# Selective-scan kernel: delta and delta*u spread by fp32 matmuls of 32 rows instead of packed bf16 parts

## What is computed

```python
s0, s1 = xf[..., diag], xf[..., anti]              # two orders of the 4096 positions
xs = jnp.stack([s0, s1, s0[..., ::-1], s1[..., ::-1]], axis=1)      # 4 directions, 192 channels
x_dbl = jnp.einsum('bkdl,kcd->bkcl', xs, x_proj_weight)
dts, Bs, Cs = jnp.split(x_dbl, [6, 22], axis=2)
delta = jax.nn.softplus(einsum('bkrl,kdr->bkdl', dts, dt_projs_weight) + dt_projs_bias)
def step(hst, inp):
    u_t, d_t, B_t, C_t = inp
    hst = hst * jnp.exp(d_t[..., None] * A) + (d_t * u_t)[..., None] * B_t[:, :, None, :]
    return (hst, jnp.einsum('bkdn,bkn->bkd', hst, C_t))
```

## Time and profile before

| | us |
|---|---|
| median of 3 runs | 16992.62 (16989.31 to 17001.06) |
| span of the profiled execution, first to last instruction | 16982.4 |
| busy: VectorE / TensorE / GpSimd / ScalarE | 14254.2 / 11990.6 / 9441.8 / 8240.7 |
| mean granted TensorE clock | 0.73 of full speed |

### The profile page before, as it was taken

One profiled execution on the slowest core, in us unless ns is written; L12 is line 12 of the kernel. 1 busy time (PEld: TensorE's weight loads), 2 busy tenths in 40 slices (PEclk: granted clock), 3 DMA queues, 4 the chain that ended last, 5 costly groups with the idle time before them and its releaser, 6 DMA issues.

```text
span 16982.4 us, 206915 instructions
## 1 busy us (share of the span) xinstructions
PE 11990.6 (71%) x50304; PEld 4377.0 (26%) x50304; DVE 14254.2 (84%) x15991; ACT 8240.7 (49%) x15277; POOL 9441.8 (56%) x4852
## 2 busy tenths in 40 slices
PE   6766777667776677766777667776677766777667
PEld 2222322223222242222422223222232222322224
DVE  6999579995799947999479995799957999579994
ACT  4555445554455534555345554455544555445553
POOL 4666346663466634666346663466634666346662
PEclk8777677776777767777677776777767777677776
DMA  1111011110111101111011110111101111011110
GB/s 31 34 33 33 17 28 33 33 33 17 27 34 33 33 17 27 34 33 33 17 27 34 33 33 17 27 33 33 33 18 27 33 33 33 19 26 33 33 33 15
DMA packets 523906, 485.87 MB, mean 29 GB/s; under 512 B 160703, under 2 KB 457312, under 8 KB 523052
## 3 DMA queue, kind: packets, MB, share of 16 engines
q1 hardware_dynamic: 523052, 476.64, 13.1%
HBM read 27.61 MB, written 12.58 MB: 2 GB/s over the span
## 4 chain that ended last, share of the span: by engine, by line
DVE 33%; issue 31%; PE 20%; ACT 7%; POOL 4%; DVEq 3%; POOLq 1%; DMA 0%; SPq 0%; ACTq 0%
DVE ps L1131 11%; DVE arena L1166 8%; PE ps L775 5%; DVE arena L1124 4%; DVE arena L1095 3%; DVE arena L1098 2%; DVE arena L1085 2%; POOL arena L467 2%; PE ps L937 2%; PE ps L936 2%; ACT arena L629 2%; PE ps L915 1%; DVE arena L1117 1%; PE ps L805 1%; POOL arena L424 1%
## 5 line engine op out<-in xcount | busy, mean ns | idle before, releaser
L467 POOL TENSOR_TENSOR arena<-arena 128x1024 f32<-128x1024 f32 x3072 | 7363.4, 2413 | 4072.1 <-PE ps L867 3764.3
L1166 DVE TENSOR_TENSOR_SCAN arena<-arena,ps 128x512 f32<-128x512 f32 x6144 | 7723.6, 1257 | 8.2
L629 ACT ACTIVATE arena<-ps,negA 128x512 f32<-128x512 f32 x6144 | 4130.8, 684 | 6261.1 <-PE ps L828 6244.4
L825 PE MATMUL ps<-arena,spread 96*128 96x512 bf16 x6144 | 2923.2, 476 | 4059.1 <-DVE arena L1166 3994.4
L1131 DVE TENSOR_TENSOR ps<-ps,arena 128x512 f32<-128x512 f32 x6144 | 4145.6, 675 | 44.3 <-PE ps L825 35.1
L867 PE MATMUL ps<-arena,gather 128*32 128x256 f32 x24576 | 3076.9, 472 | 9.5 <-POOL arena L467 9.3
L828 PE MATMUL ps<-arena,spread 96*128 96x512 bf16 x6144 | 2949.2, 480 | 12.9 <-ACT arena L629 12.9
L825 PEld LDWEIGHTS ps<-arena,spread 96*128 96x128 bf16 x6144 | 623.0, 101 | 7353.7 <-DVE arena L1166 4746.7
L424 POOL TENSOR_TENSOR arena<-arena 128x512 f32<-128x512 f32 x512 | 651.1, 1272 | 1037.7 <-ACT arena L571 1037.7
L867 PEld LDWEIGHTS ps<-arena,gather 128*32 128x32 f32 x24576 | 676.5, 119 | 1958.5 <-issue 1922.7
L805 PE MATMUL ps<-u_lo,xw_lo 128*128 (+2 forms) x1520 | 1003.7, 760 | 83.1 <-DVEq L163 54.4
(11 more groups left out here) (178 smaller groups left out, 11564.8 us busy)
## 6 DMA issues: line engine op xcount, KB each, us to landing
arena<-arena SPq DMA_DIRECT2D x3072, 96.0 KB, 2.2
arena<-arena SPq DMA_DIRECT2D x512, 256.0 KB, 5.0
arena<-in_x SPq DMA_DIRECT2D x128, 192.0 KB, 3.2
out_tokens<-arena SPq DMA_DIRECT2D x64, 192.0 KB, 2.2
arena<-in_cw SPq DMA_DIRECT2D x1, 648.0 KB
xw_lo<-in_xbc_lo SPq DMA_DIRECT2D x1, 256.0 KB
xw_hi<-in_xbc_hi SPq DMA_DIRECT2D x1, 256.0 KB
arena<-in_spread SPq DMA_DIRECT2D x1, 192.0 KB
```

The costliest lines, as they stand in the source:

```text
L467: pool.tensor_tensor(wgt[s % RW], hst[s % RH], c_rep[ch.par].unsqueeze(1).to_broadcast([P, 2, T]), ALU.mult).then_inc(weighted, 1)
L629: act.activation(decay[s % RDA][:, a, :], bank(3 + a), ACT.Exp, scale=negA[:, ch.k, group(s, a):group(s, a) + 1]).then_inc(decay_ready, 1)
L825: pe.matmul(bank(q % 3), spread[:, i, :], to_du[:, 2 * j + a, :], start=True, stop=True).then_inc(du_ready, 1)
L1166: dve.tensor_tensor_scan(hst[s % RH][:, a, flip], decay[s % RDA][:, a, flip], bank(q % 3)[:, flip], 0.0 if kind == 0 else state[:, q:q + 1 ...
```

## The change

- The tiles `delta_lo`, `du_lo` and `mixed` are doubled (by `ch.par`) and stay fp32. The parts, their splitting on VectorE, GpSimd and ScalarE, and the 12 packing DMAs are gone.
- `fill_du` and `fill_delta` take the place of `fill`: for a step, two fp32 matmuls of 32 rows each, which read the 32 channels where they lie. A tile's block of 32 channels selects the row group of the array. Even and odd steps take the two halves of the lo channels in turn, and a du fill runs one step behind the delta fill, so the two read different row groups; the hi channels come in the last four steps.
- PSUM: du in banks 0, 1 and 2, 3 by turns, delta in 4 and 5, y of lo and of hi one after the other in bank 6. `carry` for hi waits until lo is saved.
- `make_delta` reads the maximum from bank 7 instead of SBUF. `mix_du` moves to GpSimd, at its step 10, on all 128 partitions; `other_rows` waits for it.
- Gather matmuls have 512 columns instead of 2 x 256, in other places (`SUMS`); VectorE multiplies both groups of a step, then scans both.
- Rings: decays 4 steps instead of 2, weighted states 6 instead of 4; decays are issued two steps ahead.

Core of the diff:

```diff
-        SUMS = {4: (0, 1), 7: (2, 3), 8: (4,), 9: (5,), 11: (6, 7), 13: (8, 9), 14: (10,), 15: (11,)}
+        LO_STEPS = 8
+        SUMS = {3: (0, 1), 5: (2, 3), 7: (4, 5), 9: (6, 7), 11: (8, 9), NSTEP + 1: (10, 11)}
+        DU_BANKS, DELTA_BANK, Y_BANK = (0, 2), 4, 6
+        def step(ch, s):
+            return (s // 2, (s + 1 - ch.dir) % 2) if s < LO_STEPS else (s - LO_STEPS, 2)
...
+                def mix_du(ch):
+                    pool.wait_ge(delta_done, ch.n(2, 2))
...
+                    pool.tensor_tensor(mixed[ch.par], t_l, u_hi[:, bass.ds(ch.t0, T)], ALU.mult).then_inc(mixed_done, 1)
...
                 def other_rows(ch):
-                    act.wait_ge(delta_done, ch.n(2, 2))
-                    if not ch.first:
-                        act.wait_ge(split_last, ch.n(2, 0))
+                    act.wait_ge(mixed_done, ch.n(2, 1))
...
-                def fill(ch, q):
...
-                    pe.matmul(bank(q % 3), spread[:, i, :], to_du[:, 2 * j + a, :], start=True, stop=True).then_inc(du_ready, 1)
...
+                def fill_du(ch, s):
...
+                    if not (ch.first and s < 2):
+                        pe.wait_ge(scan_done, ch.n(NGRP, 2 * (s - 2) + 2))
+                    for a in range(2):
+                        tile, row = (du_lo, 32 * (2 * j + a)) if j < 2 else (mixed, ch.r0 + 32 * a)
+                        pe.matmul(bank(DU_BANKS[s % 2] + a), spread[row:row + 32, i, :], tile[ch.par][row:row + 32, :],
+                                  start=True, stop=True).then_inc(du_ready, 1)
+                def fill_delta(ch, s):
...
+                    if not (ch.first and s < 1):
+                        pe.wait_ge(decay_ready, ch.n(NGRP, 2 * (s - 1) + 2))
...
+                def carry(ch, z):
+                    if z == 1:
+                        wait_apart(pe, y_saved, ch.n(2, 1))
...
+                        if s + 2 < NSTEP:
+                            fill_du(ch, s + 2)
+                        elif nx:
+                            fill_du(nx, s + 2 - NSTEP)
+                        if s + 3 < NSTEP:
+                            fill_delta(ch, s + 3)
+                        elif nx:
+                            fill_delta(nx, s + 3 - NSTEP)
+                        if s in (3, 11):
+                            carry(ch, s // 11)
...
+                        if nx and s in (0, 5):
+                            project(nx, s // 5, 0)
+                            project(nx, s // 5, 1)
...
                     if z == 0:
-                        dve.tensor_tensor(delta_lo, t_q, t_l, ALU.max).then_inc(delta_done, 1)
...
+                        dve.tensor_tensor(delta_lo[ch.par], bank(7), t_q, ALU.max).then_inc(delta_done, 1)
```

More of the change, by code:

```diff
@@ L357, in replicate @@
                             .then_inc(bc_loaded[z], 16)
[L359 to L375, removed]
+                chunks(sp, b, lambda ch, nx, kind: replicate(nx) if nx else None, replicate)
                 rendezvous(sp, b, 2)
@@ new lines, in fill_delta @@
+                def fill_delta(ch, s):
+                    i, j = step(ch, s)
+                    if s == 0:
+                        pe.wait_ge(delta_done, ch.n(2, 1))
+                    if j == 2:
+                        pe.wait_ge(mixed_done, ch.n(2, 2))
+                    if not (ch.first and s < 1):
+                        pe.wait_ge(decay_ready, ch.n(NGRP, 2 * (s - 1) + 2))
+                    for a in range(2):
+                        tile, row = (delta_lo, 32 * (2 * j + a)) if j < 2 else (mixed, ch.d0 + 32 * a)
+                        pe.matmul(bank(DELTA_BANK + a), spread[row:row + 32, i, :], tile[ch.par][row:row + 32, :],
+                                  start=True, stop=True).then_inc(delta_ready, 1)
@@ L833, in pre @@
                         project(ch, z, 1)
-                    fill(ch, 0)
-                    fill(ch, 1)
-                def carry(ch, z, half):
+                    fill_du(ch, 0)
+                    fill_delta(ch, 0)
+                    fill_du(ch, 1)
+                    fill_delta(ch, 1)
+                    fill_delta(ch, 2)
+                def carry(ch, z):
+                    if z == 1:
+                        wait_apart(pe, y_saved, ch.n(2, 1))
+                    elif not ch.first:
+                        wait_apart(pe, y_saved, ch.n(2, 0))
                     if ch.kk == 2:
                         return
-                    if half == 0 and not ch.first:
-                        wait_apart(pe, y_saved, ch.n(2, z - 1))
-                    cols = bass.ds(ch.t0 + half * T // 2, T // 2)
+                    cols = bass.ds(ch.t0, T)
                     if z == 0:
@@ L1106, in split @@
-                def split(ch, v):
-                    if v == 0:
-                        dve.wait_ge(delta_done, ch.n(2, 1))
-                    else:
-                        dve.wait_ge(mixed_done, ch.n(2, 2))
-                    tile = (delta_lo, None, mixed)[v]
-                    if not (ch.first and v == 0):
-                        dve.wait_ge(split_first, ch.n(6, 0 if v == 0 else 2))
-                        dve.wait_ge(split_last, ch.n(2, v // 2))
-                    dve.tensor_tensor(rest, tile, first_part(tile), ALU.subtract).then_inc(split_rest, 1)
@@ L1119, in last_mixed @@
[L1119 to L1129 removed]
+                        dve.tensor_tensor(t_l[r, :], bank(7)[r, :], t_q[r, :], ALU.max).then_inc(delta_done, 1)
@@ L1146, in body @@
                     for s in range(NSTEP):
+                        multiply(ch, s)
+                        if not (ch.first and s < RH):
+                            dve.wait_ge(weighted, ch.n(NSTEP, s - RH + 1))
+                        if kind == 0:
+                            if s >= RH:
+                                dve.wait_ge(state_saved, ch.saved(s - RH + 1))
+                        elif kind == 1:
+                            dve.wait_ge(state_saved, ch.saved(ch.c * NSTEP + (s - RH + 1)))
+                        else:
+                            dve.wait_ge(state_saved, ch.saved(min(ch.c * NSTEP + s - RH + 1, (NCH - 1) * NSTEP)))
```

263 lines of the change are left out of this document (80 added, 183 removed).

## The result

The changed kernel takes **17,840 us** (median of 4 runs, 17,833.3 to 17,846.3) against 16,991 us of the kernel before on the same chip: ratio 1.050, 95% interval 1.0485 to 1.0515. It is 5% slower; the forecast was 4.4% faster. The profiled execution's span is 17,831.2 us.

What follows compares the result with a forecast made beforehand. VectorE was taken to bound the kernel: 16982.4 us less 1785 us of its work gives 15,197, plus 1042 for chunk boundaries 16,239, and with medians 10 us above the profile 16,250 us. The range was 15,400 to 17,200 us.

Steps and rivals of the forecast that it cites:

- VectorE's work: On VectorE: operations removed or moved to GpSimd and two maxima made shorter, together 1785 us less.
- The floor of the sum: Whole span if nothing but VectorE's saved work counted: 16982.4 - 1785 = 15,197 us.
- The maxima: Two VectorE operations making delta, now reading PSUM and SBUF: 0.675 us each, 346 us in all.
- Rival 4: On VectorE: a maximum with one SBUF input still waits for GpSimd; 560 us come back, 16,810 us; chance 0.03.
- A pair of fills: On TensorE: matmuls on different row groups run side by side, 1.08 us at the upper clock, 1.96 at the lower.
- Rival 3: On TensorE: row groups do not overlap, each fp32 fill costs 0.88 us by itself; 18,240 us; chance 0.15.
- The weight loads: On TensorE: four long loads per pair of new fills, 0.30 us each, a price that speaks against the change.
- Rival 2: On TensorE: loads run one after the other, a pair takes 1.5 us; 16,890 us; chance 0.16.
- The boundary of a chunk: From step 10 to step 4 of the next chunk: VectorE loses 4.2 us at each of 248, 1042 us.
- the middle, 4.2 us: Loss at each chunk boundary, taken between 3.15 us at the upper clock and 5.25 with the lower.
- The chain: Waits in a row through GpSimd, ScalarE and TensorE's in-order queue, step 10 to step 4 of the next chunk.
- under way: On TensorE at the chunk boundary: clock back up before the sums of steps 8 and 9 end at 13.9 us.

Runs made afterwards that it cites:

- e5: Kernel before, with only the maximum with the logarithm kept in PSUM and delta's two maxima reading PSUM and SBUF: 16,658 us, ratio 0.980.
- e7: Changed kernel with both fills of a pair on the same 32 rows, same count and size: 21,625 us, ratio 1.273 to the kernel before.
- e6: Changed kernel with ScalarE's decays ahead of its other work in each step and the hi rows' copy last in the chunk's list: 15,531 us, ratio 0.914.
- e8: Kernel before, with only ScalarE's decays of each step moved behind its other work of that step: 18,100 us, ratio 1.064.
- e4: Changed kernel with four unused fp32 matmuls added on TensorE at each chunk boundary, behind two added waits: 16,928 us, ratio 0.996 to the kernel before.
- e9: Changed kernel with the two waits of e4 on TensorE but none of its four matmuls: 17,816 us, ratio 1.048 to the kernel before.

## Why the prediction was wrong

**VectorE's work: right.** The floor of the sum was 15,197 us. Span less VectorE's waits at the multiplications and scans is 17,831 - 2444 - 120 = 15,267 us, 0.5% more. The maxima were put at 0.675 us and took 0.667 and 0.675. Rival 4 falls.

The Trainium skill (SBUF — State Buffer, SBUF: two separate sides) calls the port pair of VectorE and GpSimd an exclusive lock: of a VectorE instruction with two SBUF inputs and a GpSimd one that reads SBUF, the one that starts first has it to its end. 2724 ns for L1124 behind GpSimd's product and the 1.37 us of L1117 behind L431 in e5 agree with it.

**A pair of fills: right.** 1.08 us was taken, 1.13 measured at the upper clock, 1.96 and 2.08 at the lower. Du and delta fills on other row groups run beside each other as well. Rival 3, which had the sign of the result, falls as a mechanism: nothing of it happened. Its price was too low as well: it had 1250 us over the kernel before, and e7, in the order of the change, came to 4636.

**The weight loads: hidden.** A load of 32 rows and 128 columns takes 222 and 231 ns on average (L766, L780), one of 128 rows and 128 columns in the same kernel 215 and 235 (L751, L747), so the rule of the Trainium skill that columns alone count (TensorE: Matmul & The Clock Gate, LDWEIGHTS (loading the stationary operand)) agrees with the trace. But the four loads of a pair, 0.19 us each at the upper clock, stand as 0.30 us in all, and the pair takes 1.13 us: on two row groups they overlap. Rival 2 falls.

**The boundary of a chunk: the step that failed.** "I take the middle, 4.2 us", 1042 us in all. Measured were 9.9 us a boundary, 2462 us in all, as means over the 248:

| step | foretold, upper and lower clock | found |
|---|---|---|
| 0 | 0.35, 0.35 | 0.47 |
| 1 | 0.15, 1.95 | 1.92 |
| 2 | 1.75, 2.05 | 3.39 |
| 4 | 0.9, 0.9 | 2.50 |
| 10 | nothing | 1.64 |

The chain was the right one as far as it went, and its first two steps were right at the lower clock. Four things were mis-sized.

- It took a middle between the two clocks and left the upper clock half of the weight. The rows had the idle times beside the slow lines, and TensorE stood 4.5 us: there was no ground for the upper clock. At step 1 this is 0.9 us.
- At step 2 the clock was let up "under way". It came later than that: delta fill, carry and sums of steps 8 and 9 were given 5.0 us (8.9 to 13.9) and took 7.4 in the chunk at 407 (407.21 to 414.59). The chunk at 1242 has 2.36 us at step 2 and seems to confirm the 2.05, but by luck: the carry that the sum counts isn't there.
- At step 4 the clock was taken as up. Where it was, the wait is the foretold one (0.81 us in the chunk at 476; 0.8 to 1.0 in 46 of the 248). Mostly the sums of steps 10 and 11 ran in part or all at the lower clock, 3.25 us in the chunk at 1258 where 1.76 were counted, and the wait was 2.4 to 2.7 us in 130 chunks and 4.0 to 4.2 in 64.
- The chain has a second copy. The other projection, clamp and logarithm stand before the decays of steps 8 and 9 in the same way, and VectorE loses 1.64 us at step 10. The text followed the chain "from step 10 to step 4" and stopped.

With the 101 us of the first chunks and 70 us at the floor, the 1420 us that the boundaries cost above the sum make the whole miss of 1590 us.

Behind all four is a part of the change that was costed only where it touched that chain, and that the list of the change doesn't name: ScalarE's decays moved from the head of each step to its end. The prediction treated the decays two steps ahead as a cover. But the delta fill is only one step ahead, in one pair of banks, and waits for the decays; through TensorE's queue in order everything behind waits as well. e6 and the changed kernel differ in ScalarE's order alone, and one is 8.6% faster, the other 5% slower than before; e8 shows that the order costs 6.4% in the kernel before.

**Why the range missed.** Each of its cases let the order stand and varied TensorE's price. A rival "the waits repeat at the other projection, at the lower clock" was missing. Twice the chain with the lower figure would have given 10.5 us a boundary, 2604 us, 17,811 us, but that is near the result by luck: the second copy costs 1.64 us, not 5.25, and steps 2 and 4 make up for it.

What stays open: what sets the clock in a given chunk, and the kernel of e6 with added matmuls, which wasn't tried.

## To carry to other kernels

When a change moves an engine's instructions past each other, cost each move for itself: what does the moved one feed, and how far ahead is the consumer's *narrowest* buffer (here one pair of PSUM banks, not the ring of four decays)? Put what feeds the next engine first, and what only waits for others last. Follow a chain of waits through the whole period, not to its first end, and look at more than one kind of chunk before a wait is taken for the rule. Price what stands behind an idle time of TensorE at both clocks, all the way along: the same wait of 1.63 us was followed by the one in some chunks and by the other in others.

## What the runs showed of the hardware

- Four fp32 fills of 32 rows, 128 columns and 512 positions on four row groups, two and two issued apart, took 1.14 us together at the upper clock (1251.10 to 1252.24 in the changed kernel's timeline), about as long as the one full fp32 matmul behind them (L747, 1.13 us); with one row group for each pair the kernel is 3785 us slower.
- Useless matmuls can pay: 992 of them in an idle stretch raised the granted clock of a scan phase from 0.77 to 0.86 and took 888 us off (e4 against e9).
- Being busy did not keep the upper clock in e7: from 1280 to 1300 us TensorE was busy for 20.00 us, and the granted clock was 0.50.
- Freeing a VectorE operation from GpSimd's port gave 331 of 576 us; a neighbour that still reads two SBUF tiles took over 170 us of the wait, 1.37 instead of 0.66 us each time it met GpSimd's instruction (e5).
